# Attention values in three column blocks, ones on a sum of two key tiles, moves by DMA

## The chip, the cores and the metric

The kernel runs on one core of a Trainium2 chip. Its engines are TensorE (PE), VectorE (DVE), ScalarE (ACT), GpSimd (POOL) and SyncE (SP, which here only issues DMAs); each has its own queue and they meet by semaphores. The metric is the device time of one launch in microseconds, the median of several runs.

## The reference

A block of adaptive layer norm, causal attention and a mixture of experts on x of 4 x 2048 x 512, in fp32. Cut to what the change touches:

```python
h = _layernorm(x) * (1 + ca) + sa
qkv = h @ Wqkv.T + bqkv; q, k, v = split(qkv)      # 16 heads of 32 channels
q, k = _rope(q), _rope(k)
att = einsum('bhqd,bhkd->bhqk', q, k) / sqrt(32)
att = softmax(where(causal, att, -inf), axis=-1)
y = einsum('bhqk,bhkd->bhqd', att, v)
x = x + ga * (y @ Wo.T + bo)
h = _layernorm(x) * (1 + cb) + sb
x = x + gb * moe(h)                                # 48 of 128 experts kept, top 8
```

## The kernel before

A batch of 2048 tokens is worked through in three stages, and a loop runs over the 4 batches. **The front**: norm, projections of q, k and v with weights split in two fp32r parts (`W`), rotation; q and k go to DRAM (`qkd`), v to DRAM (`vd`) and for the first group of four heads to SBUF (`V`). **The stream**: attention of 16 heads, one after another. **Routing**: output projection (L1209), second norm, gates. At the end of the stream all five engines meet (`meet`, L568 by the helper), and again at the end of routing. After the last batch come the 48 experts.

In the stream the scores are computed transposed: 128 keys on the partitions, a chunk `j` of 512 queries in the columns. A head has four chunks; chunk j has 4(j+1) key tiles, so a head has 40 tiles, taken in 20 units of two. Each tile is one product into PSUM (L1160, with a mask product at the diagonal, L1163), one exponential on ACT into a ring `Pt` (L999), and one product with the values (L1181). Four heads share a group `g`: their results lie in four blocks of 32 partitions of `ot`. The denominators of the softmax come from ones that stand beside the values in `V`: `values_and_ones` gives 64 columns, 32 of values and 32 of ones. The first tile of a unit writes PSUM partitions 0 to 63, the second 64 to 127 (L1181).

At the end of a chunk ACT copies four blocks of 32x512: values and denominators of the first tiles straight to `ot` and `den`, those of the second tiles to `od` (L984 to L988); POOL adds `od` to them (L876, L877). At the end of a group DVE inverts `den` (L1442), POOL multiplies (L885) and SP stores `ot` to DRAM (`otd`). Beside this the maxima of the next head are found: a product per tile (L1136), a reduction on DVE (L1417, L1421), a transpose (L1141), and two rows of maxima that SP copies into the q operand (L661). They are needed by the scores of chunks 0 and 2. The last head of a batch has no next one, and so no maxima beside it.

The order is written out by hand in `stream()`: in step n every engine takes the score of unit n, the value of unit n-2, what is in `beside[n]` (maxima) and in `closing[n]` (copies, additions, inverses, scaling, `fold` and `widen`). `fold` multiplies the output weights by the gate (L858), `widen` adds the bias to two chunks of tokens `xc` (L866). SP has an order of its own, a loop over heads (L626 onwards): wait for the scores of the last head, 12 loads of the next (`stack`), row of maxima, stores, row of maxima, and after the last head the loads of attention and tokens for two output chunks (`load_attention`, L724, and `load_tokens`, L728).

Of the kernel before, what the change touches and what calls it, by code (L numbers as in the profile page):

```python
# [7 lines left out]
F32 = mybir.dt.float32  # L8
F32R = mybir.dt.float32r
BF16 = mybir.dt.bfloat16  # L10
# [5 lines left out]
P = 128  # L16
# [78 lines left out]
NPT = 8  # L95
# [4 lines left out]
def extent(j, k):  # L100

    r = max(k - TPC * j, 0)
    first = 0 if (j, k) == (0, 1) else r * P
    return first, (r + 1) * P - first if k >= TPC * j else 0

# [36 lines left out]
def stream():  # L142
# [27 lines left out]
    for n in range(NU * H):  # L170
        out.append(("score", *divmod(n, NU)))
        if n >= 2:
            out.append(("value", *divmod(n - 2, NU)))
        out += beside[n] + closing[n]
    for n in range(NU * H, NU * H + 16):
        if n < NU * H + 2:
            out.append(("value", *divmod(n - 2, NU)))
        out += closing[n]
# [3 lines left out]
NV, NPT_B = NU * H, 2 * NU * H  # L182
# [65 lines left out]
def adaln_block(nc, x, wqkv, bqk, bv, wo, bo, cT, wmod, gwT, o2n_col, o2n_row, wgu, wdn, cos, sin, kst, out):  # L248
    with ExitStack() as ctx:
# [13 lines left out]
        qkd = dram("qkd", [NB, NG, P, 4, T])  # L263
        vd = dram("vd", [NB, P, NT, NG * P])
# [19 lines left out]
        idbf = place("idbf", [P, P], BF16)  # L284
        mtbf = place("mtbf", [P, 2 * P], BF16)
# [11 lines left out]
        V_AT = at[0]  # L297
        V = place("V", [P, 2, NT, 6, HD], F32)
# [4 lines left out]
        PT_AT = at[0]  # L303
        Pt = place("Pt", [P, NPT, CH], F32)
        OD_AT = at[0]
        od = place("od", [P, 2, 2, CH], F32)
        den = place("den", [P, T], F32)
        ot = place("ot", [P, T], F32)
# [16 lines left out]
        rsA = place("rsA", [P, TPC], F32)  # L325


        at[0] = X_AT = PT_AT + 2 * NPT * CH
        xin = [place("xin0", [P, TPC, C], F32), xin1]
        assert at[0] <= OD_AT  # L330
# [6 lines left out]
        vst = [vst0, place("vst1", [P, TPC, NG * P], F32)]  # L337
# [8 lines left out]
        at[0] = V_END - 4 * NT * 6 * HD  # L346
# [39 lines left out]
        B1 = place("B1", [P, TPC, 6, P], BF16)  # L386
# [3 lines left out]
        assert at[0] <= X_AT  # L390


        at[0] = OD_AT
# [8 lines left out]
        posi = place("posi", [P, TPC, NEW], I32)  # L402
        hi = place("hi", [P, TPC, NEW], I32)
        lo = place("lo", [P, TPC, NEW], I32)
        assert at[0] <= FRONT_AT - 4 * T
# [51 lines left out]
        w_lower = sem("w_lower")  # L457
        cs_in = [sem("cs_in0"), sem("cs_in1")]
# [27 lines left out]
        o_norm = sem("o_norm")  # L486
        den_inv = sem("den_inv")
        ot_ready = sem("ot_ready")
# [82 lines left out]
        def o_part(h, j, odd, what):  # L571

            at = 2 * odd + (what + h) % 2
            return O[j % 2][at * HD:(at + 1) * HD, :]

        def values_and_ones(g, k, h):

            at = h // 2 * 3 + h % 2
            return V[:, g % 2, k, at:at + 2, :].rearrange("p a d -> p (a d)")

# [4 lines left out]
        def _(sp):  # L585
# [17 lines left out]
            wait_apart(sp, mod_out, 80)  # L603

            with sp.Fori(0, NB) as b:
# [30 lines left out]
                def slots_of(g, tiles, heads):  # L636

                    return ((V[:, g % 2, tiles, 0, :], heads[:, :, 0:HD]),
                            (V[:, g % 2, tiles, 2:4, :].rearrange("p t a d -> p t (a d)"), heads[:, :, HD:3 * HD]),
                            (V[:, g % 2, tiles, 5, :], heads[:, :, 3 * HD:P]))  # L640

                def store_values(j):

                    wait_apart(sp, s1_dve, N_DVE * b + EMPTIED["vproj", j, TPC - 1])
                    sp.dma_start(vd[b, :, TPC * j:TPC * (j + 1), :], vst[j % 2][:, :, :]).then_inc(v_out[j % 2], 16)
                    if j == 0:
                        wait_apart(sp, ones_set, 5 * b + 3)
# [1014 lines left out]
```

## Time and profile before

| | us |
|---|---|
| median of 3 runs | 4691.33 |
| lowest, highest | 4687.53, 4701.44 |
| the profiled execution | 4692.54 |
| its span, first to last instruction | 4690.7 |
| mean granted TensorE clock | 0.941 of 2.4 GHz |

The profile is one execution of the program. The span is shared by the engines; busy time of PE covers matmuls whose ends are modelled, and weight loads (PEld) overlap them. The chain of waits is followed back from the last instruction: at each step to what released it. Idle time of an engine outside that chain costs nothing. The names of DMAs and instructions are output<-input.

### The profile page before, as it was taken

The page shows a single profiled execution, that of the slowest core. Times are in us where ns is not written, and L with a number is a line of the kernel's source. Part 1 is how long each engine was busy: PE and PEld are TensorE (multiplying, and loading weights), DVE is VectorE, ACT ScalarE, POOL GpSimd, SP SyncE. Part 2 cuts the span into 40 slices and gives each one's busy share as a digit, 9 for nine tenths or more (in the row PEclk, how much of TensorE's full clock was granted, in tenths as well). Part 3 has the DMA queues.
Part 4 walks back from the last instruction along what each step waited for, and adds up shares of the span by engine and source line. Part 5 has one row for each costly group of instructions (what it writes and reads, how often), then busy time and mean ns, then how long its engine had stood idle before and what let it go on. Part 6 is the DMA issues. An engine that isn't in the chain of part 4 may idle for free.

```text
span 4690.7 us, 75544 instructions
## 1 busy us (share of the span) xinstructions
PE 4213.7 (90%) x18784; PEld 2336.3 (50%) x18784; DVE 2924.8 (62%) x5831; ACT 2293.1 (49%) x4294; POOL 1584.6 (34%) x1059
## 2 busy tenths in 40 slices
PE   4899999886899999886899999867899999859998
PEld 2744444345744444355644444346644444337776
DVE  3766666565756667475657766475666666465655
ACT  1347767622356677532267677422377676321111
POOL 3632223313622223314522223305522223304544
PEclk8989999997989999987899999988899999979999
DMA  4431222122432122123412222123422221229997
GB/s 138 147 112 57 57 66 71 52 88 89 161 86 64 46 58 70 58 97 113 157 49 66 62 69 57 64 96 115 147 52 66 66 65 42 93 75 248 259 253 196
DMA packets 325089, 460.75 MB, mean 98 GB/s; under 512 B 143540, under 2 KB 150836, under 8 KB 321972
## 3 DMA queue, kind: packets, MB, share of 16 engines
q1 hardware_dynamic: 303160, 397.48, 27.9%
q0 software_dynamic: 21504, 58.40, 5.3%
q8 instruction: 168, 2.75, 0.2%
q14 instruction: 257, 2.11, 0.1%
HBM read 292.99 MB, written 168.56 MB: 98 GB/s over the span
## 4 chain that ended last, share of the span: by engine, by line
PE 64%; issue 16%; POOL 6%; DMA 5%; DVE 4%; ACT 3%; SPq 1%; POOLq 1%; ACTq 0%; DVEq 0%
PE PS L1181 23%; PE PS L1136 14%; PE PS L1160 11%; PE PS L1283 3%; PE PS L1209 3%; DMA out<-z,it 2%; POOL qs L850 2%; PE PS L1294 2%; POOL t L847 2%; PE PS L1163 1%; ACT Pt L999 1%; POOL hTl L823 1%; PE PS L1222 1%; PE PS L1254 1%; PE PS L1120 1%
## 5 line engine op out<-in xcount | busy, mean ns | idle before, releaser
L999 ACT ACTIVATE Pt<-PS 128x512 f32<-128x512 f32 (+3 forms) x2560 | 1230.9, 533 | 778.6 <-PE PS L1163 401.0
L1421 DVE TENSOR_REDUCE part<-PS 128x1 f32<-128x512 f32 x1536 | 1019.3, 686 | 715.9 <-PE PS L1136 715.3
L1181 PE MATMUL PS<-Pt,V 128*64 128x512 f32 (+3 forms) x5120 | 1276.0, 560 | 0.0
L1136 PE MATMUL PS<-QK 96*128 96x512 f32 (+3 forms) x2560 | 865.1, 420 | 68.2 <-DVE part L1421 34.1
L876 POOL TENSOR_TENSOR ot<-ot,od 32x512 f32<-32x512 f32 x256 | 326.1, 1274 | 1726.1 <-ACT od L985 1726.1
L1160 PE MATMUL PS<-QK 97*128 97x512 f32 (+3 forms) x2560 | 828.0, 391 | 24.1 <-ACT Pt L999 9.4
L1136 PEld LDWEIGHTS PS<-QK 96*128 96x128 f32 x2560 | 396.2, 192 | 892.3 <-DVE part L1417 416.4
L1417 DVE CUSTOM_DVE_ANT_0 PS<-PS,consts 128x128 f32<-128x128 f32 (+3 forms) x1024 | 500.9, 495 | 145.8 <-PE PS L1136 142.8
L1160 PEld LDWEIGHTS PS<-QK 97*128 97x128 f32 x2560 | 481.2, 193 | 162.7 <-ACT Pt L999 56.4
L1181 PEld LDWEIGHTS PS<-Pt,V 128*64 128x64 f32 x5120 | 255.9, 135 | 311.9 <-issue 240.3
L1120 PE MATMUL PS<-hTu,W 128*128 128x512 f32 x1024 | 349.8, 425 | 18.3 <-POOL hTl L823 18.3
L877 POOL TENSOR_TENSOR den<-den,od 32x512 f32<-32x512 f32 x256 | 324.0, 1266 | 0.0
L1442 DVE RECIPROCAL den<-den 128x128 f32<-128x128 f32 x256 | 235.6, 936 | 101.8 <-POOL den L877 101.8
L956 ACT ACTIVATE qraw<-PS,bqg 128x512 f32<-128x512 f32 x128 | 87.2, 688 | 380.8 <-PE PS L1120 237.1
L1283 PEld LDWEIGHTS PS<-XT,Wg 128*96 128x96 f32 x1536 | 250.6, 164 | 26.6 <-issue 25.4
L1283 PE MATMUL PS<-XT,Wg 128*96 128x192 f32 x1536 | 259.1, 327 | 1.3 <-ACT XT L1045 1.3
L1209 PE MATMUL PS<-wot,otc 128*128 128x512 f32 x384 | 193.1, 643 | 64.9 <-POOLq L568 64.9
L1120 PEld LDWEIGHTS PS<-hTu,W 128*128 128x128 f32 x1024 | 209.6, 208 | 66.1 <-issue 19.6
L1163 PE MATMUL PS<-mtbf,idbf 128*128 128x128 bf16 (+1 forms) x1024 | 234.6, 237 | 0.0
L850 POOL TENSOR_TENSOR qs<-qs,cs 128x1024 f32<-128x1024 f32 x64 | 211.2, 3301 | 30.5 <-DVE qs L1397 30.5
L847 POOL TENSOR_TENSOR t<-qraw,cs 128x1024 f32<-128x1024 f32 x64 | 155.5, 2430 | 179.5 <-ACT qraw L956 179.5
L1120 PE MATMUL PS<-hTl,W 128*128 128x512 f32 x512 | 215.0, 420 | 0.0
(161 smaller groups left out, 4743.4 us busy)
## 6 DMA issues: line engine op xcount, KB each, us to landing
QK<-qkd SPq DMA_DIRECT2D x720, 128.0 KB, 3.0
qkd<-st SPq DMA_DIRECT2D x64, 1024.0 KB, 4.4
Wg<-wgu SPq DMA_DIRECT2D x48, 768.0 KB
Wd<-wdn SPq DMA_DIRECT2D x48, 384.0 KB
xin<-x SPq DMA_DIRECT2D x16, 1024.0 KB, 5.4
vd<-vst SPq DMA_DIRECT2D x16, 1024.0 KB, 6.0
table<-modd SPq DMA_DIRECT2D x64, 256.0 KB, 4.0
xc<-x SPq DMA_DIRECT2D x16, 1024.0 KB, 7.6
```

The source lines that it names most:

```text
L850: nc.gpsimd.tensor_tensor(qs[:, :, :], qs[:, :, :], table_of, ALU.mult).then_inc(rope_mul, 1)
L876: nc.gpsimd.tensor_tensor(ot[own, cols], ot[own, cols], od[own, nn % 2, 0], ALU.add)
L877: nc.gpsimd.tensor_tensor(den[own, cols], den[own, cols], od[own, nn % 2, 1], ALU.add).then_inc(o_norm, 1)
L999: nc.scalar.activation(Pt[:, t % NPT, first:CH], S2[t % NS2][:, first:CH], ACT.Exp, scale=SCALE).then_inc(exp_done, 1)
L1120: last = mm(bank, W[:, w, k, i, g * P:(g + 1) * P], (hTu, hTl)[h][:, j % 2, k], start=(k, w, h) == (0, *TERMS[0]), stop=(k, w, h) == (KT - ...
L1136: mm(s1[:, 0:w], QK[0:3 * HD, hh % 2, 0, qb * P:(qb + 1) * P], QK[0:3 * HD, hh % 2, 1, c * CH:c * CH + w], start=True, stop=True).then_inc ...
L1160: last = mm(S2[t % NS2][:, first:CH], QK[0:3 * HD + 1, hh % 2, 1, k * P:(k + 1) * P], QK[0:3 * HD + 1, hh % 2, 0, j * CH + first:(j + 1) * ...
L1181: last = mm(O[j % 2][2 * i * HD:2 * (i + 1) * HD, first:CH], values_and_ones(g, kb + i, hh % GH), Pt[:, (2 * n + i) % NPT, first:CH], star ...
L1209: last = mm(PS[:, t % 2], rows_of, wot[:, k, :], start=k == 0, stop=k == KT - 1)
L1283: last = mm(banks[i][:, q, :], Wg[:, u % HELD, k, o:o + HALF], XT[:, u % 2, k // 2, k % 2, :], start=k == 0, stop=k == KT - 1)
L1417: v.tensor_tensor_reduce(out=s1[:, 0:w], in0=s1[:, 0:w], in1=K[:, K_NEG + CH - w:K_NEG + CH], scale=1.0, scalar=-3e38, op0=ALU.add, op1=AL ...
L1421: v.reduce_max(part[:, qb, cc:cc + 1], s1[:, 0:w], AX.X).then_inc(s1_dve, 1)
```

## The change

A unit becomes a round. Its two value products have 32 columns each and write partitions 0 to 31 and 32 to 63 of the bank. POOL adds the two probability tiles into `Sm` (step `plus`, new), and one product with a tile of ones `onesv` writes the denominators to partitions 96 to 127; at the diagonal the columns that only the first tile has get a ones product of their own. `V` has no more ones in it. The value of a round stands three units behind its score (LAG) instead of two, and `Pt` has 12 places instead of 8. At a chunk's end ACT copies the whole bank to `od` in one instruction, and SP moves three blocks of 32 partitions to their rows: to `ot`, to a new `o1` (the second tiles) and to `den`. Per group and chunk POOL adds `o1` to `ot` (step `join`).

`Pt`, `Sm` and `o1` lie where `W` was. So the split weights are stored to DRAM (`wd`) once, before the loop over batches, and loaded back in each routing stage.

```diff
+SHAPES = ((2,) * 2, (2,) * 4, (2,) * 6, (2,) * 8)
-NPT = 8
+NPT, NSM, LAG = 12, 3, 3
@@ stream()
-        closing[n + 2].append(("copy", hh, j, 0))
-        closing[n + 3] += [("copy", hh, j, 1), ("add", hh, j)]
+        closing[n + LAG].append(("copy", hh, j))
         if hh % GH == GH - 1:
+            closing[n + 7].append(("join", hh // GH, j))
             for i in range(TPC):
-                closing[n + 6 + i].append(("inverse", hh // GH, j, i))
-            closing[n + 6 + TPC].append(("scale", hh // GH, j))
+                closing[n + 7 + i].append(("inverse", hh // GH, j, i))
+            closing[n + 7 + TPC].append(("scale", hh // GH, j))
+            due[NU * hh + DUE[r]].append(("value", hh, r))
+            beside[min(NU * hh + DUE[r] - LAG, NU * H - 1)].append(("plus", hh, r))
@@ sync, before the loop over batches
             wait_apart(sp, mod_out, 80)
+            wait_apart(sp, w_lower, 1)
+            sp.dma_start(wd, W[:, :, :, :, :].bitcast(F32)).then_inc(w_out, 16)
+            wait_apart(sp, w_out, 16)
@@ sync, values of the first group
-                    for slot_of, heads in slots_of(0, slice(TPC * j, TPC * (j + 1)), vst[j % 2][:, :, 0:P]):
-                        sp.dma_start(slot_of, heads).then_inc(v_out[j % 2], 16)
+                    sp.dma_start(V[:, 0, own, :], vst[j % 2][:, :, 0:P]).then_inc(v_out[j % 2], 16)
+                def move(hh, j):
+                    nn = NCH * hh + j
+                    own, cols = slice(hh % GH * HD, (hh % GH + 1) * HD), slice(j * CH, (j + 1) * CH)
+                    wait_apart(sp, o_free, NCH * H * b + nn + 1)
+                    for slot_of, whole in ((0, ot), (1, o1), (3, den)):
+                        sp.dma_start(whole[own, cols], od[slot_of * HD:(slot_of + 1) * HD, nn % 2]).then_inc(o_moved[nn % 2], 16)
@@ sync, loop over heads: after the 12 loads of the next head
+                    if hh >= 2:
+                        move(hh - 2, NCH - 1)
                     max_row(hh - 1, 1)
+                    move(hh - 1, 0)
...
+                    move(hh - 1, 1)
                     if hh < H:
                         max_row(hh, 0)
...
+                    move(hh - 1, 2)
...
+                move(H - 1, NCH - 1)
@@ sync, routing
+                sp.dma_start(W[:, :, :, :, :].bitcast(F32), wd).then_inc(w_in, 16)
@@ gpsimd
+                    elif kind == "plus":
+                        pool.wait_ge(exp_done, ...)
+                        if at >= NSM:
+                            pool.wait_ge(pv_done, ONE + NV * b + at - NSM + 1)
+                            nc.gpsimd.tensor_tensor(total, of[0][:, first:CH] if i == 1 else total, of[i][:, first:CH], ALU.add).then_inc(sum_done, 1)
+                    elif kind == "join":
+                        pool.wait_ge(o_moved[nn % 2], ...)
+                        nc.gpsimd.tensor_tensor(ot[:, cols], ot[:, cols], o1[:, cols], ALU.add).then_inc(joined, 1)
@@ scalar
-                            nc.scalar.activation(od[own, nn % 2, 0], o_part(hh % GH, j, 1, 0), ACT.Copy)
-                            nc.scalar.activation(od[own, nn % 2, 1], o_part(hh % GH, j, 1, 1), ACT.Copy).then_inc(o_free, 1)
-                            nc.scalar.activation(ot[own, cols], o_part(hh % GH, j, 0, 0), ACT.Copy)
-                            nc.scalar.activation(den[own, cols], o_part(hh % GH, j, 0, 1), ACT.Copy)
+                        nc.scalar.activation(od[:, nn % 2], O[j % 2], ACT.Copy).then_inc(o_free, 1)
@@ tensor
-                        for i in range(2):
-                            last = mm(O[j % 2][2 * i * HD:2 * (i + 1) * HD, first:CH], values_and_ones(g, kb + i, hh % GH),
-                                      Pt[:, (2 * n + i) % NPT, first:CH], start=kb == 0, stop=kb == TPC * j + 2)
+                        for i, k in enumerate(ks):
+                            mm(O[j % 2][i * HD:(i + 1) * HD, firsts[i]:CH], V[:, g % 2, k, h * HD:(h + 1) * HD], of[i][:, firsts[i]:CH],
+                               start=begins, stop=r == LAST_USE[j, i])
+                        if firsts[1] > firsts[0]:
+                            mm(O[j % 2][3 * HD:P, firsts[0]:firsts[1]], onesv[:, :], of[0][:, firsts[0]:firsts[1]], start=begins, stop=False)
+                        mm(O[j % 2][3 * HD:P, firsts[1]:CH], onesv[:, :], Sm[:, at % NSM, firsts[1]:CH], start=begins, stop=r == LAST_ROUND[j]).then_inc(pv_done, 1)
```

How instructions stand now, at three places. First PE's queue in a steady head, around a value step at the diagonal. Before (L1136 maxima, L1160 scores, L1181 values):

```order
L1136 MATMUL PS<-QK 128x512 [waits s1_dve]
L1159 REGISTER_ALU
L1160 MATMUL PS<-QK 128x512 [waits exp_done]
L1159 REGISTER_ALU
L1160 MATMUL PS<-QK 128x512 [waits exp_done]
L1181 MATMUL PS<-Pt,V 64x256 [waits exp_done]
L1181 MATMUL PS<-Pt,V 64x128
```

After (L1166 maxima, L1190 scores, L1214 values, L1217 and L1218 ones):

```order
L1166 MATMUL PS<-QK 128x512 [waits s1_dve]
L1189 REGISTER_ALU
L1190 MATMUL PS<-QK 128x512 [waits exp_done]
L1189 REGISTER_ALU
L1190 MATMUL PS<-QK 128x512 [waits exp_done]
L1199 REGISTER_ALU
L1214 MATMUL PS<-Pt,V 32x256 [waits sum_done]
L1214 MATMUL PS<-Pt,V 32x128
L1217 MATMUL PS<-Pt,onesv 32x128
L1218 MATMUL PS<-Sm,onesv 32x128
```

Two products of 64 columns gave way to four of 32 here (off the diagonal to three), and the step waits for POOL's sum, where it waited for the exponential.

Second SP's queue at the end of a batch, from its last wait for a head's scores. Before:

```order
L562 REGISTER_ALU [waits s2_ready]
L661 DMA QK<-mT 1x8x128 [waits mt_ready]
L710 ISA
L710 DMA table<-modd 128x512
L562 ISA
L724 DMA otc<-otd 128x512 [waits ot_out0]
L724 DMA otc<-otd 128x512 x2
L728 DMA xc<-x 128x4x512
L724 DMA otc<-otd 128x512 [waits ot_out1]
L724 DMA otc<-otd 128x512 x2
L728 DMA xc<-x 128x4x512
```

After, from the moves of the last head's last chunk:

```order
L595 REGISTER_ALU
L684 DMA ot<-od 32x512 [waits o_free]
L684 DMA o_87<-od 32x512
L684 DMA den<-od 32x512
L595 ISA
L760 DMA otc<-otd 128x512 [waits ot_out0]
L760 DMA otc<-otd 128x512 x2
L764 DMA xc<-x 128x4x512
L760 DMA otc<-otd 128x512 [waits ot_out1]
L760 DMA otc<-otd 128x512 x2
L764 DMA xc<-x 128x4x512
```

The loads of attention (`otc`) and tokens (`xc`) stood right behind the last row of maxima; now they stand behind the last move, which waits for the last head's copy.

Third POOL's queue at the same place. Before, from the additions of the last chunk (L876, L877), and after, from the last sum (L911); L866 and L896 widen the tokens, L885 and L925 scale:

```order
L876 TENSOR_TENSOR ot<-ot,od 32x512 [waits o_free]
L877 TENSOR_TENSOR den<-den,od 32x512
L864 REGISTER_ALU [waits o_norm]
L865 ISA [waits gabo]
L866 TENSOR_TENSOR xc<-xc,rows 128x2048 [waits c_in0]
L866 TENSOR_TENSOR xc<-xc,rows 128x2048 [waits c_in1,gabo,o_norm]
L884 ISA [waits o_norm]
L885 TENSOR_TENSOR ot<-ot,den 128x512 [waits den_inv]
```

```order
L911 TENSOR_TENSOR Sm<-Pt 128x128 [waits pv_done]
L924 ISA [waits joined]
L925 TENSOR_TENSOR ot<-ot,den 128x512 [waits den_inv]
L894 REGISTER_ALU
L895 ISA [waits gabo]
L896 TENSOR_TENSOR xc<-xc,rows 128x2048 [waits c_in0]
L918 TENSOR_TENSOR ot<-ot,o_87 128x512 [waits o_moved1]
L896 TENSOR_TENSOR xc<-xc,rows 128x2048 [waits c_in1,gabo]
L924 ISA [waits joined]
L925 TENSOR_TENSOR ot<-ot,den 128x512 [waits den_inv]
```

The additions are gone; the widening of the second chunk now stands behind the joining of the last one (L918), and the joining behind the widening of the first.

## Rows read from the trace of the kernel before

**Rows 1.** Page: busy time by engine, and the chain that ended last, by engine.
```profile
PE 4213.7 (90%) x18784; PEld 2336.3 (50%) x18784; DVE 2924.8 (62%) x5831; ACT 2293.1 (49%) x4294; POOL 1584.6 (34%) x1059
...
PE 64%; issue 16%; POOL 6%; DMA 5%; DVE 4%; ACT 3%; SPq 1%; POOLq 1%; ACTq 0%; DVEq 0%
```

**Rows 2.** Windows: us; busy PE, PEld, DVE, ACT, POOL (count); clock; DMA share; GB/s.
```profile
496.00:536.40 40.40, 40.35 (x178) 17.97 (x178) 24.31 (x60) 28.57 (x57) 10.03 (x8) 1.00 0.17 46
...
890.60:925.40 34.80, 32.80 (x135) 11.90 (x133) 13.92 (x22) 27.68 (x54) 12.64 (x11) 1.00 0.34 114
```

**Rows 3.** Chain of waits, 570 to 580 us: start, us, engine and line.
```profile
570.04 1.01 PE PS L1181 x4
...
571.94 0.58 PE PS L1181 x3
```

**Rows 4.** Timeline of PE from 945 us: start us, us, engine, line, op.
```profile
949.03 1.02 PE L1209 MATMUL PS<-wot,ot 128*128 128x512 f32 x2
...
952.47 1.02 PE L1209 MATMUL PS<-wot,ot 128*128 128x512 f32 x2
```

**Rows 5.** Groups by line and form: two weight loads of PE.
```profile
L1181 PEld LDWEIGHTS PS<-Pt,V 128*64 128x64 f32 x5120 | 255.9, 135 | 311.9 <-issue 240.3 <-ACT Pt L999 33.9
...
L1141 PEld LDWEIGHTS PS<-consts,mx 128*8 128x8 f32 x128 | 10.6, 83 | 88.4 <-issue 77.6 <-DVE mx L1427 10.8
```

**Rows 6.** Timeline of POOL, the folding of the output weights.
```profile
803.56 4.97 POOL L858 TENSOR_TENSOR wot<-wot,rows 128x512 f32<-128x512 f32 x4
```

**Rows 7.** Groups by line and form: one of four copies on ACT.
```profile
L985 ACT ACTIVATE od<-PS 32x512 f32<-32x512 f32 x256 | 150.9, 589 | 3.0
```

**Rows 8.** Timeline of PE in a batch's last head.
```profile
919.90 0.50 PE L1160 MATMUL PS<-QK 97*128 97x512 f32 x1 [0.38 <-ACT Pt L999]
```

**Rows 9.** Timeline of SP's queue in a steady head.
```profile
564.15 7.03 SPq L626 DMA_DIRECT2D QK<-qkd  x12
...
574.74 0.72 SPq L661 DMA_DIRECT2D QK<-mT  x1
```

**Rows 10.** Chain of waits at the program's start.
```profile
66.65 3.92 DMA out<-zrow
...
70.89 0.44 SPq L608
```

**Rows 11.** DMA issues: count, size, median us to landing.
```profile
wm<-wmod SPq DMA_DIRECT2D x1, 6144.0 KB, 17.7
...
qkd<-st SPq DMA_DIRECT2D x64, 1024.0 KB, 4.4
```

**Rows 12.** Chain of waits at the hand-over into the stream.
```profile
271.98 4.32 DMA V<-vst
```

**Rows 13.** Timeline of PE at the same place.
```profile
281.10 0.77 PE L1136 MATMUL PS<-QK 96*128 96x128 f32 x2 [4.21 <-DMA QK<-qkd]
```

**Rows 14.** Timeline of all engines at a batch's end.
```profile
925.40 2.36 PE L1181 MATMUL PS<-Pt,V 128*64 128x512 f32 x12
...
930.36 1.26 POOL L876 TENSOR_TENSOR ot<-ot,od 32x512 f32<-32x512 f32 x1 [3.77 <-ACT od L985]
...
933.08 8.95 POOL L866 TENSOR_TENSOR xc<-xc,rows 128x2048 f32<-128x2048 f32 x2 [0.24 <-POOL den L877]
...
941.98 1.26 POOL L885 TENSOR_TENSOR ot<-ot,den 128x512 f32<-128x512 f32 x1
```

**Rows 15.** Timeline of SP's queue, loads for the output stage.
```profile
899.23 1.31 SPq L724 DMA_DIRECT2D otc<-otd  x3
...
900.63 0.39 SPq L728 DMA_DIRECT2D xc<-x  x1
...
903.10 0.62 SPq L728 DMA_DIRECT2D xc<-x  x1
```

**Rows 16.** Line L728 (token loads) from 890 to 915 us.
```profile
DMA to landing us min/median/max: 7.6/8.7/9.8
```

**Rows 17.** Waits: PE for the row of maxima.
```profile
PE PS L1160 <- DMA QK<-mT: 0.6, 1, 0.6
```

More of the change, by code:

```diff
@@ L94 @@
 ENDS = [max(u for u in range(NU) if UNITS[u][0] == j) for j in range(NCH)]
-NPT = 8
+SHAPES = ((2,) * 2, (2,) * 4, (2,) * 6, (2,) * 8)
+ROUNDS = [(j, tuple(range(sum(shape[:r]), sum(shape[:r + 1])))) for j, shape in enumerate(SHAPES) for r in range(len(shape))]
+NR = len(ROUNDS)
+NPT, NSM, LAG = 12, 3, 3
 NS1 = NS2 = 3
@@ L104, in extent, with tile_at @@
     return first, (r + 1) * P - first if k >= TPC * j else 0
+def tile_at(j, k):
+    return 2 * j * (j + 1) + k
+FIRST_ROUND = [min(r for r in range(NR) if ROUNDS[r][0] == j) for j in range(NCH)]
+LAST_ROUND = [max(r for r in range(NR) if ROUNDS[r][0] == j) for j in range(NCH)]
+DUE = [tile_at(j, ks[-1]) // 2 + LAG for j, ks in ROUNDS]
+LAST_USE = {(j, i): r for r, (j, ks) in enumerate(ROUNDS) for i in range(len(ks))}
+N_SUM = sum(len(ks) - 1 for _, ks in ROUNDS)
+SUMS = [sum(len(ks) - 1 for _, ks in ROUNDS[:r + 1]) for r in range(NR)]
+ROUND_OF = {tile_at(j, k): r for r, (j, ks) in enumerate(ROUNDS) for k in ks}
 def front():
@@ L169, in stream, with moved @@
     out = []
[L170 to L177, printed above, removed]
+    for n in range(NU * H + 16):
+        if n < NU * H:
+            out.append(("score", *divmod(n, NU)))
+        out += due[n]
+        if n < NU * H:
+            out += beside[n]
         out += closing[n]
     return out
-NV, NPT_B = NU * H, 2 * NU * H
+NV, NPT_B = NR * H, 2 * NU * H
+def moved(nn):
+    return 16 * sum(3 for m in range(nn % 2, nn + 1, 2))
 STEPS = front() + stream()
@@ L284, in adaln_block @@
         idbf = place("idbf", [P, P], BF16)
+        onesv = place("onesv", [P, HD], F32)
         mtbf = place("mtbf", [P, 2 * P], BF16)
@@ L389, in adaln_block @@
         pos = place("pos", [P, TPC, NEW], F32)
-        assert at[0] <= X_AT
-        at[0] = OD_AT
+        posi = place("posi", [P, TPC, NEW], I32)
+        assert at[0] <= OT_AT
+        at[0] = SPARE_AT
+        B1 = place("B1", [P, TPC, 6, P], BF16)
         B2 = place("B2", [P, TPC, 6, 2, P], BF16)
@@ L485, in adaln_block @@
         o_free = sem("o_free")
-        o_norm = sem("o_norm")
+        sum_done = sem("sum_done")
+        joined = sem("joined")
+        o_moved = [sem("o_moved0"), sem("o_moved1")]
         den_inv = sem("den_inv")
-        ot_ready = sem("ot_ready")
+        ot_ready = [sem("ot_ready%d" % j) for j in range(NCH)]
         ot_out = [sem("ot_out%d" % j) for j in range(NCH)]
@@ L1176, in _ @@
-                        if kb == 0 and nn >= 2:
-                            pe.wait_ge(o_free, ONE + NCH * H * b + nn - 1)
-                        for i in range(2):
-                            first, _ = extent(j, kb + i)
-                            last = mm(O[j % 2][2 * i * HD:2 * (i + 1) * HD, first:CH], values_and_ones(g, kb + i, hh % GH),
-                                      Pt[:, (2 * n + i) % NPT, first:CH], start=kb == 0, stop=kb == TPC * j + 2)
-                        last.then_inc(pv_done, 1)
+                        _, hh, r = step
```

156 lines of the change are left out of this document (74 added, 82 removed).

## The prediction

> **What bounds the kernel now.** I read the page first: TensorE (PE) is busy for 90% of a span of 4690.7 us and the chain of waits lies on it for 64% [rows 1]. That is a mean over stages, so the windows come next. In a steady head of the attention stream (one head is 20 units of two key tiles and takes 40.4 us; there are 16 heads and 4 batches) PE is busy for 40.35 of 40.40 us at full clock (2.4 GHz), while ScalarE (ACT) works 28.57 and GpSimd (POOL) 10.03 [rows 2]. Only the last head of a batch, which has no maxima to find beside it, leaves PE idle: 32.80 of 34.80 us [rows 2]. So in 15 of 16 heads a change pays only if it takes columns, loads or array changes from PE. The chain inside one head shows what a unit costs: a value group with 512 columns holds the chain for 1.01 us, one with 256 and 128 columns for 0.58 [rows 3]. Around the stream other things set the end: the start of the program, the hand-over into the stream, and the end of each batch, where all engines meet.
>
> **The value products.** Before, the two tiles of a unit go to two blocks of 64 columns side by side (values and ones in one product). After, they go to two blocks of 32, and a third block of 32 takes ones times the sum of the two probability tiles. Does that cut streaming? An fp32 product of 512 columns is two instructions; four such products with the whole array take 3.43 us from the start of one row to the next but one, 0.86 each [rows 4]. A unit's two products take 1.01 together, so the two blocks already run side by side and only 0.15 us is load and change of shape. A third block beside them saves no column. What gets shorter is the first weight load: 8 columns take 83 ns and 64 take 135 [rows 5], 0.93 ns per column, so 32 fewer save 30 ns. Against that stand the start of a third block (two more instructions and two more loads) and, in 7 of 20 units, a split of the ones product at the diagonal. No row shows a third block. From below: nothing added, -30 ns a unit. From above: the second block, the load and the change of shape cost 0.15 together, so +0.07 if a further block takes half of that. I take +16, since a unit of 1.01 leaves little that a second block can have cost, so -14 ns net. Times 20 x 64 = 1280 units: **-18 us** (-38 to +90).
>
> The Trainium skill weighs here ("TensorE: Matmul & The Clock Gate", "Measured speedup vs the span model"): further blocks add about 4 ns each, but the same table gives three column blocks 2.38 times the speed of one, not 3. No row has three blocks; two agree with the first figure. By the first, the estimate for this term would be -33 us; by the second a unit would take 3/2.38 of 0.86, which is 1.08, and the term would be +90 us (estimate).
>
> **The sums.** 20 additions per head on POOL, of 128x512 where the unit is off the diagonal. Four POOL products of that shape take 4.97 us [rows 6], 1.24 each, so at most 25 us a head beside PE's 40.4; the 8 additions of 32 rows that go took 10. The product of unit n now stands three units later instead of two, so a sum has nearly two units (4 us) for its 1.24: hidden. The reductions on DVE read PSUM. Once a batch the folding of the output weights occupies POOL for 4.97 + 1.24 us [rows 6], three units; the sums behind it come about half a microsecond late: **+2 us** over four batches (0 to 6).
>
> **The copies.** Per chunk four ACT copies of 32x512 at 589 ns [rows 7] become one of 128x512, which takes as long: 7 us of ACT less per head. In a steady head PE idles 0.05 us, so nothing comes of it. In the last head PE waits for the exponentials behind these copies, seven times, 0.2 to 0.4 us; one of them is [rows 8]. All 2.0 us of idle time [rows 2] may go: **-8 us** for four batches (0 to -12).
>
> **The moves.** 12 more DMAs per head on SP's queue. The 12 loads of the next head take SP 7.03 us from 564.15 [rows 9], 0.59 each, so it is past them at 571.2. The value group at 570.04 [rows 3] will be the one that closes the previous head; its copy, behind two exponentials, is done near 572. Three moves at 0.59 last until 573.8, and the row of maxima for which SP waits next is issued at 574.74 [rows 9]. They fit with 0.9 us to spare: 0.
>
> **Start of the program.** The split weights are now written to DRAM once (6144 KB), after zeroing is done, and SP waits for that before it loads any input. The chain runs through SP at just this place: it waits 3.92 us for the DMA on `out`, and at 70.89 issues the first input [rows 10]. Nothing hides it. The load of the same size took 17.7 us; a write of 1024 KB takes 4.4 [rows 11], which six times over is 26, and 15 if 2 us of each are fixed. **+18 us**, once. Reading it back comes after the meeting, where its space is free and the next use is a whole routing stage away: 0.
>
> **Hand-over into the stream.** SP stores the last values with four DMAs, waits for all, and only then loads head 1. The last of the three DMAs with small elements ends that chain, 4.32 us to land [rows 12], and PE idles 4.21 us [rows 13]. Now it is one DMA with 512 byte pieces. I take 1.5 us each time: **-6 us** (0 to -12).
>
> **End of each batch.** This is the largest term. Before, from the last value product (ends at 925.40 + 2.36 = 927.76): copies, two additions, then POOL adds the bias to two token chunks (8.95 us), scales the last chunk and all engines meet; 941.98 + 1.26 is 15.5 us after the product [rows 14]. The tokens had been loaded 30 us earlier, issued at 900.63 and 903.10 [rows 15]. After, SP must issue the moves of the last head first; the attention and token loads stand behind the very last move (SP's order shows it). Counted from the last product: copy 0.7, SP and three moves 1.7 to 1.9, so the first attention load is issued at 2.4. From there the first tokens land 1.40 + 7.6 = 9.0 later [rows 15, 16]: 11.4. Widening one chunk, 4.47 [rows 14]: 15.9. Joining, 1.24: 17.1. Second widening (its tokens land at 2.4 + 3.87 + 9.8 = 16.1): 21.6. Scaling, 1.26: 22.9. Against 15.5 that is +7.4, four times: **+30 us** (20 to 40). What had been covered by POOL's own work, the tokens' landing, becomes the wait that ends last.
>
> **Sum.** -18 + 2 - 8 + 18 - 6 + 30 = +18. Own time of the profiled execution 4692.5 (1.8 outside the span); it lies 1.2 above the median of 4691.33. Forecast 4710.5, so **4710 us**, 0.4% slower. About 0.3% (14 us) is what a measurement can tell from no change: 4677 to 4705 counts as the same.
>
> **Rivals.**
> *The third block does not run fully beside the others.* The array takes the third block's columns in turns: three blocks take 1.5 times two. Place: every value group. 16 units of 512 columns at +0.43 us and 4 of 256 at +0.21 give 7.7 us a head, 493 in all: 5200 us. A milder form (+0.07 a unit, the upper bound above) gives 4710 + 108 = 4818. (The page's 2.38 would be this form.) For it: no row has three blocks. Against: two run together at no visible price. Chance 0.08 and 0.06.
> *Faster: the change of shape gets cheaper too.* The 0.15 us of a unit is load and drain. If both shrink with the columns of a block, half of it, 75 ns a unit, goes: -96 instead of -18, so 4632. Place: again the value groups. It decides from 28 ns a unit (36 us of other terms over 1280). For it: only the 0.15 that the rows leave unexplained. Against: the load of 64 columns is 60 ns of it at 0.93 each [rows 5], and a wait for the array to drain need not know columns. With a part of it, 4660 to 4690. Chance 0.15.
> *A new wait in the stream.* The row of maxima that SP sends at 574.74 is needed by the first score of the third chunk, four units after the score that precedes the group at 570.04 [rows 3], so near 577.5; it held PE once already, for 0.6 us [rows 17]. If the moves take longer to issue than the loads, or their packets delay its landing, PE waits 0.5 to 1 us in 60 heads: +30 to +60, so 4740 to 4770. Chance 0.16.
> *Forecast as written:* 0.55, with 4692 to 4730 as its own range.
>
> **Numbers.** Below 4677: most of the second rival, 0.11. From 4677 to 4705: its rest and a quarter of the forecast's case, in which the two large losses are nearer their lower bounds, 0.27. Above: 0.62. The range leaves out the first rival in both forms and the far end of the second: 4678 to 4790.
>
> **What would show it.** Value groups of 512 columns near 1.00 us in the chain (rival one: 1.08 to 1.43). PE in a steady head still above 99% busy, period 40 us. In the last head no wait of PE for ACT. First input DMA issued near 89 us instead of 71. From the last value product to the last scaling 23 us instead of 15, with POOL's wait before the first widening put down to the DMA of the tokens. A wait of PE for the row of maxima would show the third rival. I am wrong if the value groups shrink by more than 28 ns or grow.

## The result, and the profile after

The changed kernel takes **4715.71 us** (median of 11 runs, 4704.89 to 4726.96); the kernel before, on the same chip, 4694.53 (11 runs, 4687.53 to 4703.12). The ratio is 1.0049 [1.0037, 1.006], so it is slower, by about half a per cent. The profiled spans are 4710.5 and 4690.7: 19.8 us to account for; the medians are 21.2 apart. The page after, answering [rows 1], busy time and the chain:

```profile
PE 4168.9 (89%) x22240; PEld 2362.4 (50%) x22240; DVE 2910.1 (62%) x5832; ACT 1818.7 (39%) x3526; POOL 2378.9 (51%) x1883
...
PE 67%; issue 15%; POOL 8%; DVE 4%; DMA 3%; ACT 1%; SPq 1%; POOLq 1%; DVEq 0%; ACTq 0%
```

ACT lost 474 us of work, POOL took 794, and PE, which counts, lost 45. The windows answer [rows 2]: a steady head, then the last head of the first batch.

```profile
496.00:536.40 40.40, 40.16 (x238) 18.51 (x232) 24.48 (x62) 21.42 (x46) 21.46 (x20) 1.00 0.27 70
901.80:934.00 32.20, 31.51 (x190) 12.24 (x188) 14.04 (x22) 20.31 (x42) 23.46 (x22) 1.00 0.14 34
```

Read the second number against the first: PE still fills a steady head to 99.4%, and in the last head it now idles 0.7 us where it idled 2.0.

To place the 19.8 us, take three kinds of instants from PE's timeline in each batch: the first transposes, the last score and the first output product. The first column below is when the program's first transposes start; the next two are means of the four batches, from a batch's first score to its last (the stream), and from there to the first output product (the end of the batch). "Routing" is all that follows the first output product, summed over batches, the experts at the program's end included. Each kernel is told of below. The four stage columns come from one profiled execution of each kernel, which lies up to 15 us from its median; each ratio is to the kernel before on the same chip.

| kernel | start | stream | end of batch | routing, sum | median us | ratio to before |
|---|---|---|---|---|---|---|
| before | 82.5 | 662.8 | 18.9 | 1162 | 4694.5 | |
| after | 99.0 | 655.5 | 28.5 | 1157 | 4715.7 | 1.0049 [1.0037, 1.006] |
| e1, loads before the moves | 99.2 | 666.0 | 16.3 | 1161 | 4704.5 | 1.0026 [1.0016, 1.0036] |
| e2, start without the wait | 83.7 | 655.5 | 28.0 | 1172 | 4709.4 | 1.0033 [1.0021, 1.0046] |
| e3, four blocks | 98.8 | 657.8 | 28.1 | 1153 | 4722.5 | 1.0075 [1.0061, 1.0089] |
| e4, ones once a chunk | 98.7 | 653.1 | 27.8 | 1166 | 4708.4 | 1.0036 [1.0022, 1.005] |
| e5, loads between the moves | 99.2 | 655.7 | 18.0 | 1163 | 4680.8 | 0.9973 [0.9963, 0.9984] |
| e6, two tiles, repaired | 83.4 | 656.0 | 14.3 | 1163 | 4650.3 | 0.9908 [0.9893, 0.9924] |
| e7, three tiles | 99.4 | 631.3 | 32.9 | 1147 | 4625.4 | 0.9859 [0.9843, 0.9876] |
| e8, three tiles, repaired | 83.2 | 629.9 | 17.4 | 1163 | 4568.2 | 0.9734 [0.9721, 0.9747] |
| e9, joins on DVE | 83.1 | 653.3 | 19.5 | 1161 | 4669.6 | 0.996 [0.9945, 0.9975] |
| e10, joins later | 83.6 | 631.2 | 17.9 | 1172 | 4570.5 | 0.9754 [0.9737, 0.9772] |

After against before: start +16.5, four streams -29.1, four ends +38.4, routing -5.5, the stages before the streams -0.5; sum +19.8. The change works where it was aimed and pays for it at the edges.

**Start.** The chain there, answering [rows 10]:

```profile
66.66 3.89 DMA out<-zrow
70.70 15.93 DMA wd<-W
```

**Value groups.** The chain of waits in a steady head, start and duration; one group, first the first of the two instructions of each product, then the second:

```profile
511.61 0.55 PE PS L1214 x2
512.16 0.01 PE PS L1218
512.17 0.42 PE PS L1214 x2
512.59 0.01 PE PS L1218
```

The four pieces make 0.99 us against the 1.01 of [rows 3]. The blocks of 32 (L1214 values, L1218 ones) lie over each other, and no column is paid for twice. The first load, answering [rows 5], takes 27 ns less:

```profile
L1214 PEld LDWEIGHTS PS<-Pt,V 128*32 128x32 f32 x5120 | 184.8, 108 | 333.5 <-issue 204.8 <-POOL Sm L911 48.3 <-ACT od L1017 43.6
```

Counted from one group's first weight load to the next instruction's, in twelve steady heads of each batch, the median group of 512 columns went from 1009 to 989 ns, one split at the diagonal from 1009 to 994, the narrow one from 576 to 568. One narrow group in each head takes 0.88 us after the change, because the product behind it waits 0.3 us for DVE; the scores near it take 0.3 us less than before. The steady heads as wholes went from 40.49 to 40.16 us (medians), which agrees with the medians of the groups.

**End of a batch.** The timeline answers [rows 14, 15]. Follow it down: last sum, last value product, copy, three moves, and only then the loads.

```profile
936.21 1.28 POOL L918 TENSOR_TENSOR ot<-ot,o 128x512 f32<-128x512 f32 x1
937.44 0.47 POOL L911 TENSOR_TENSOR Sm<-Pt 128x128 f32<-128x128 f32 x1
937.96 0.40 PE L1214 MATMUL PS<-Pt,V 128*32 128x256 f32 x2 [0.57 <-POOL Sm L911]
938.66 0.60 ACT L1017 ACTIVATE od<-PS 128x512 f32<-128x512 f32 x1 [3.90 <-PE PS L1218]
940.53 0.59 SPq L684 DMA_DIRECT2D den<-od  x1
942.82 0.39 SPq L764 DMA_DIRECT2D xc<-x  x1
949.81 4.49 POOL L896 TENSOR_TENSOR xc<-xc,rows 128x2048 f32<-128x2048 f32 x1 [10.68 <-DMA xc<-x]
954.26 1.26 POOL L918 TENSOR_TENSOR ot<-ot,o 128x512 f32<-128x512 f32 x1
955.47 4.49 POOL L896 TENSOR_TENSOR xc<-xc,rows 128x2048 f32<-128x2048 f32 x1
959.92 1.26 POOL L925 TENSOR_TENSOR ot<-ot,den 128x512 f32<-128x512 f32 x1
961.90 2.90 PE L1244 MATMUL PS<-wot,otc 128*128 128x512 f32 x3 [23.30 <-POOLq L601]
```

From the last value product's end (938.6) to the last scaling's end (961.2) is 22.6 us, forecast at 22.9. What I had not counted is at the top: the join of chunk 2 (936.21) stands in POOL's queue ahead of the last sum, so the last value product itself comes late (it waits 0.57 us, and its weight load 1.26). From the last score to its end, 2.7 us became 4.7.

### The profile page after: what moved, and what is told of

Read it like the earlier page. It is cut to its first block, busy times and chain, and to the rows that moved or that the text cites. A ratio compares the mean times of both kernels' runs of the same rounds, so it can differ in the third digit from the quotient of the medians.

```text
span 4710.5 us, 86803 instructions
## 1 busy us (share of the span) xinstructions
PE 4168.9 (89%) x22240; PEld 2362.4 (50%) x22240; DVE 2910.1 (62%) x5832; ACT 1818.7 (39%) x3526; POOL 2378.9 (51%) x1883
## 3 DMA queue, kind: packets, MB, share of 16 engines
q14 instruction: 282, 2.31, 0.2%
## 4 chain that ended last, share of the span: by engine, by line
PE 67%; issue 15%; POOL 8%; DVE 4%; DMA 3%; ACT 1%; SPq 1%; POOLq 1%; DVEq 0%; ACTq 0%
PE PS L1214 21%; PE PS L1166 15%; PE PS L1190 11%; PE PS L1318 5%; PE PS L1329 3%; PE PS L1244 3%; POOL qs L884 3%; PE PS L1218 2%; POOL t L881 2%; PE PS L1193 1%; POOL hTl L859 1%; PE PS L1257 1%; PE PS L1289 1%; PE PS L1304 1%; DMA xc<-x 1%
## 5 line engine op out<-in xcount | busy, mean ns | idle before, releaser
L911 POOL TENSOR_TENSOR Sm<-Pt 128x512 f32<-128x512 f32 (+2 forms) x1280 | 1370.6, 1074 | 1054.8 <-PE PS L1218 833.4
L1214 PE MATMUL PS<-Pt,V 128*32 128x512 f32 (+3 forms) x5120 | 1242.5, 547 | 7.4 <-POOL Sm L911 7.0
L1218 PE MATMUL PS<-Sm,onesv 128*32 128x512 f32 (+2 forms) x2560 | 1130.6, 524 | 0.0
L1166 PE MATMUL PS<-QK 96*128 96x512 f32 (+3 forms) x2560 | 866.6, 420 | 88.3 <-DVE part L1457 33.9
L1190 PE MATMUL PS<-QK 97*128 97x512 f32 (+3 forms) x2560 | 808.2, 388 | 13.7 <-DVE vst L1426 8.7
L1166 PEld LDWEIGHTS PS<-QK 96*128 96x128 f32 x2560 | 398.0, 192 | 839.4 <-DVE part L1453 351.4
L1190 PEld LDWEIGHTS PS<-QK 97*128 97x128 f32 x2560 | 478.4, 194 | 121.7 <-ACT Pt L1028 38.4
L1150 PE MATMUL PS<-hTu,W 128*128 128x512 f32 x1024 | 349.2, 424 | 17.9 <-POOL hTl L859 17.9
L1214 PEld LDWEIGHTS PS<-Pt,V 128*32 128x32 f32 x5120 | 184.8, 108 | 333.5 <-issue 204.8
L951 POOL DMA_INDIRECT out<-z,it x96 | 139.3, 1451 | 213.2 <-issue 128.8
```

What stands on the lines that cost most here:

```text
L911: nc.gpsimd.tensor_tensor(total, of[0][:, first:CH] if i == 1 else total, of[i][:, first:CH], ALU.add).then_inc(sum_done, 1)
L1150: last = mm(bank, W[:, w, k, i, g * P:(g + 1) * P], (hTu, hTl)[h][:, j % 2, k], start=(k, w, h) == (0, *TERMS[0]), stop=(k, w, h) == (KT - ...
L1166: mm(s1[:, 0:w], QK[0:3 * HD, hh % 2, 0, qb * P:(qb + 1) * P], QK[0:3 * HD, hh % 2, 1, c * CH:c * CH + w], start=True, stop=True).then_inc ...
L1190: last = mm(S2[t % NS2][:, first:CH], QK[0:3 * HD + 1, hh % 2, 1, k * P:(k + 1) * P], QK[0:3 * HD + 1, hh % 2, 0, j * CH + first:(j + 1) * ...
L1214: mm(O[j % 2][i * HD:(i + 1) * HD, firsts[i]:CH], V[:, g % 2, k, h * HD:(h + 1) * HD], of[i][:, firsts[i]:CH], start=begins, stop=r == LAS ...
L1218: mm(O[j % 2][3 * HD:P, firsts[1]:CH], onesv[:, :], Sm[:, at % NSM, firsts[1]:CH], start=begins, stop=r == LAST_ROUND[j]).then_inc(pv_done, 1)
```

## The experiments

### e1: the loads before the last head's moves

```diff
                     max_row(hh - 1, 1)
+                    if hh == H:
+                        for j in range(2):
+                            load_attention(j)
+                            load_tokens(j)
                     move(hh - 1, 0)
...
                 move(H - 1, NCH - 1)
...
-                for j in range(2):
-                    load_attention(j)
-                    load_tokens(j)
```

> SP issues the attention and token loads of the first two chunks in the last head ahead of that head's first moves, not behind its very last one; nothing else changes. Theory (the end of a batch grew by 28.5 - 18.9 = 9.6 us because the tokens land late): the first widening no longer waits for them. From the last score: last value product 4.7, then copy and moves to 9.3 (2.4 us and 2.0 to land), join 1.3, scaling 1.3, but POOL's two widenings of 4.5 each stand in front of them as in the kernel before, so about 19 to 20 us to the first output product, 8.5 less per batch, 34 in all: 4680 us. Rival (the three moves with their own 2 us landing, and the joins, are what ends last, not the tokens): 2 to 3 us per batch at most, 4705 to 4710.

Measured: 4704.5. The end of a batch fell by 12.2 us, below that of before. But the last head grew from 32.1 us (first to last score) to 40.1 to 45.1. The line of the moves from 905 to 945 us (who waited for it, and its time to landing), then a row of PE's waits there:

```profile
its engine sat idle before it (us, times) until:
who waited for it (us, times):
  DVE den L1480: 25.6, 2
  POOL ot L919: 9.0, 1
...
DMA to landing us min/median/max: 1.9/4.6/10.3
```
```profile
PE PS L1215 <- POOL Sm L912: 7.7, 1, 7.7
```

The moves of 64 KB landed in up to 10.3 us instead of 2.0: they stood behind 3.5 MB of loads (two chunks of 1024 KB of tokens and 768 KB of attention; the expectation of e5 miscounts them as 2.8). POOL's join waited 9.0 for them, the sums stood behind the join, and PE waited 7.7. The clock then cost more. Windows of 10 us around and behind that wait (the second number is PE's busy time, the third from the end the granted clock):

```profile
925.00:935.00 10.00, 2.31 (x8) 0.32 (x8) 4.33 (x6) 1.09 (x2) 3.85 (x4) 0.66 0.44 133
935.00:945.00 10.00, 10.00 (x36) 3.51 (x36) 2.93 (x4) 4.65 (x9) 7.50 (x6) 0.50 0.08 20
```

PE was busy for 2.31 of 10 us, and all of the next 10 us ran at 1.2 GHz (0.50). So a wait of 7.7 us goes with a head that is 13 us longer. The median of 4704.5 lies at the rival's edge, but not by the rival's mechanism: the end of a batch fell by 12.2, not by 2 to 3. That the tokens' landing is what ends last is the theory's; e5 shows it without the longer head. Why the place was wrong, neither had.

### e5: the loads between the moves

The same four lines, behind `move(hh - 1, 1)`.

> The loads of attention and tokens for the first two chunks stand behind the last head's moves of its second chunk (in the queue of SP), so that the moves of the first two chunks land ahead of them. Theory (what ends last at the end of a batch is the landing of the tokens, and e1 lost 8 to 15 us in the last head only because three moves stood behind 2.8 MB in the same DMA queue): stream 655.5 us as in the changed kernel, last score to first output product 16 to 17 us instead of 28.5; 12 us x 4 = 48, 4668 us. Rival (any 2.8 MB in the last head holds the moves up and with them POOL's joins and sums): the stream grows by 8 us or more again, 4700 us or above.

Measured: 4680.8, faster than before. The stream is 655.7, as in the changed kernel, and the end of a batch 18.0, 10.5 less (12 forecast). This one edit of order turns the change from a loss of 0.5% to a gain of 0.3%, which is small but clear of its interval. The rival's first half does show: the moves still behind the loads landed in up to 6.4 us. No join and no sum of POOL waited for them, though, so the rival is out.

### e2: the start without the wait

```diff
-            sp.dma_start(wd, W[:, :, :, :, :].bitcast(F32)).then_inc(w_out, 16)
-            wait_apart(sp, w_out, 16)
...
                 sp.dma_start(bvg[:, :], bv.rearrange("g p -> (g p)").partition_broadcast(P)).then_inc(bv_in, 16)
+                sp.dma_start(wd, W[:, :, :, :, :].bitcast(F32)).then_inc(w_out, 16)
...
+                wait_apart(sp, w_out, 16 * (b + 1))
                 sp.dma_start(W[:, :, :, :, :].bitcast(F32), wd).then_inc(w_in, 16)
...
+                            if t == 0:
+                                act.wait_ge(w_out, ONE + 16 * (b + 1))
```

> The 6144 KB write of the split weights is issued behind the first input loads of a batch, in every batch, and ScalarE waits for it before the first exponential instead of SP at the program's start. Theory: the start gets its 16 us back (first transposes at 83 instead of 99 us), nothing else moves: 4700 us. Rival (the transfers share bandwidth, the write delays the second input or the stores of the first parts in each of four batches): part of the 16 is given back, up to 10 us per batch, and it comes out between 4700 and 4740.

Measured: 4709.4. The first transposes start at 83.7, 15.3 us earlier, and streams and ends are as they were; the stages before the streams too (718.9 against 718.5 us, summed over batches), so the rival's delay isn't there. Of the forecast 16 us, 6 came in the medians and 1.2 in the profiled executions. What is missing there lies in the routing stage, where this edit adds one wait of SP for a write that had long landed: 1172 against 1157 us. The windows of that stage in the first batch, of after and of e2:

```profile
961.90:1133.20 171.30, 123.20 (x617) 80.22 (x617) 110.27 (x222) 39.15 (x60) 16.07 (x9) 0.83 0.37 131
```
```profile
947.90:1121.90 174.00, 125.17 (x617) 80.82 (x617) 114.42 (x222) 39.29 (x60) 16.06 (x9) 0.81 0.38 133
```

The same 617 instructions run at a mean granted clock of 0.83 and 0.81. Over the twelve kernels the routing sum lies between 1147 and 1172 us, so much of this is scatter that comes with the clock. It isn't shown that the edit has no part in it: the five kernels that carry it (e2, e6, e8, e9, e10) have sums of 1161 to 1172, the seven others 1147 to 1166. That stays open.

### e3 and e4: a block more, a block less

```diff
+                        for slot_at in (2, 3):        # e3: both get ones times the sum
...
+                        if begins:                    # e4: ones in a chunk's first group alone
```

> Each value group gets a fourth block: ones times the sum once more, into the 32 partitions that nobody reads. Theory (a block beside others costs only its start and its load, 16 us ns-scale as in the prediction, +16 ns a unit): group of 512 columns 989 to about 1005 ns, 16 x 1280 ns = +20 us, 4736 us. Rival of turns (blocks share the array's input): +0.43 us a group of 512, +493 us, above 5200; its mild form +0.07 us a unit, 4805. If the fourth block costs nothing at all, 4716.

> Leaves out the denominators: ones are multiplied in the first group of each chunk only (with constant data), so 16 of the 20 groups per head have two blocks of 32 columns and nothing else. Theory (load term -30, third block +16): these groups fall from 989 to about 973 to 979 ns, 10 to 16 ns x 1024 groups = 10 to 16 us less, 4700 to 4705. Rival A (the third block costs nothing, the gain is all load or something else): 989 stays, 4716. Rival B (the third block costs as much as a share of the columns): over 50 ns a group, under 4665.

Measured: 4722.5 and 4708.4 (4736 and 4700 to 4705 forecast); median group of 512 columns 996 ns with four blocks, 989 with three, 982 with two. The chain of e4 has the group in one piece, for the reader to compare with the pieces of after:

```profile
508.40 0.98 PE PS L1214 x4
```

(The 16 in the expectation of e3 are ns.) The medians are counted from weight load to weight load, as above. e4 leaves out most of the denominators. Streams grew by 2.3 us with the fourth block and fell by 3.0 to 4.2 in three batches of e4; its second batch was 0.8 longer, with three heads 0.3 to 1.6 us above those of the others. So a block beside others costs **7 ns**, not 16. And two blocks of 32 take 27 ns less than before's two blocks of 64: exactly the difference of the two weight loads, 135 to 108. Nothing is left for a drain that would depend on the columns of a block. Both forms of turns (+0.43 and +0.07 us) are excluded, and so is the faster rival. The two figures of the Trainium skill ("TensorE: Matmul & The Clock Gate", "Measured speedup vs the span model") part here: its 4 ns for a further block is the nearer one, and low against the 7 measured, and its 2.38 times for three blocks doesn't show in this kernel, where the measured group of 989 decides against the 1080 that it would give.

### e6: both repairs, and the second widening behind the meeting

> The edit of e5, the edit of e2 (write of the split weights behind the first input loads, waited for by ScalarE), and the widening of the second token chunk moved behind the meeting of the engines. Theory: 48 from the tokens, 16 from the start, and 4.5 x 4 = 18 from the widening, which stands on POOL ahead of the last join and scaling: 4716 - 82 = 4634 us. Rival (the last moves, 2.4 us behind the last value product and 2.0 to land, set the end once the tokens are early, and the widening hides behind them): 4640 to 4652.

Measured: 4650.3. The last edit takes 3.7 us off each end of a batch (18.0 to 14.3; 4.5 forecast). Of the 82 us, 65 came; 9 are missing from the ends (57 instead of 66), 6 are in the routing stage, 2 lie in the streams. The total is in the rival's range, but its mechanism doesn't show in the first batch: POOL begins the last join as soon as it is done with the first widening, and doesn't wait for the moves. That first widening still stands ahead of the join.

### e7 and e8: three key tiles in a group

If a block costs 7 ns, the fourth quarter of the array stands empty for nothing. A third tile in a group saves whole groups.

```diff
-SHAPES = ((2,) * 2, (2,) * 4, (2,) * 6, (2,) * 8)
+SHAPES = ((2, 2), (3, 3, 2), (3, 3, 3, 3), (3, 3, 3, 3, 2, 2))
...
+        o2 = place("o2", [P, T], F32)
-                    for slot_of, whole in ((0, ot), (1, o1), (3, den)):
+                    for slot_of, whole in ((0, ot), (1, o1), *([(2, o2)] if j else []), (3, den)):
```

> Value groups of three key tiles where the chunk has enough of them: 15 groups per head instead of 20, with a fourth block (third tile) in 10 of them, one more sum per group on POOL (25 per head), one more move per chunk and one more addition at the end; the row of maxima is sent ahead of the previous head's last moves. Theory (a block beside others costs 7 ns, a group 0.98 us): per head 16 groups of 0.99 and 4 of 0.57 become 11 of 1.00, one of 0.79 and 3 of 0.57, 18.1 to 13.5, so 4.6 x 64 = 297 us less, 4419 us. Rival A (PE no longer bounds: POOL's 25 sums of 1.07 and ScalarE's 40 exponentials in 35.6 us make PE wait half a microsecond or more in every third group): 4480 to 4560. Rival B (the row of maxima comes too late for a head of 35.6 us): 1 to 2 us a head, 4480 to 4540.

> The groups of e7 with the three repairs of e6. Theory: the two gains add, 4419 - 82 = 4337 us. Rival (with the shorter last head the loads of the tokens collide with the moves, as in e1): up to 8 us per batch of it is lost, 4370 us.

Measured: 4625.4 and 4568.2; **e8 is 2.7% faster than the kernel before**. A clear gain, but e7 brought 90 us where 297 were forecast, less than either rival allowed; e8 brought 57 of its 82. The value groups did shrink as worked out: median 996 ns at 512 columns, 14.0 us of them per head against 18.4. Heads fell only from 40.2 to 37.1, and those in which a group of heads closes (numbers 3, 7 and 11, counted from 0) to between 39.9 and 42.5. Windows of e8, an ordinary head and the one from 403 us, in which a group closes:

```profile
497.00:534.10 37.10, 36.12 (x218) 17.34 (x210) 23.81 (x61) 20.86 (x44) 27.08 (x25) 1.00 0.31 78
403.00:440.00 37.00, 34.08 (x195) 15.98 (x194) 28.87 (x64) 19.08 (x39) 32.49 (x28) 0.95 0.24 63
```

In the first PE idles 1.0 us: groups are fewer, the scores and maxima between them as many, and PE waits for the banks that DVE empties and for the row of maxima. In the second POOL works 32.5 of 37.0 us, nearly without a gap from 411 to 439, with the sums of the group behind its joins and scalings. DVE is nearly as full in places. Two windows of 5 us of that head, and two of the last head of the same batch:

```profile
425.00:430.00 5.00, 3.05 (x17) 1.22 (x15) 4.79 (x10) 2.67 (x5) 4.92 (x4) 0.98 0.37 106
430.00:435.00 5.00, 5.00 (x20) 2.24 (x20) 2.09 (x4) 1.49 (x3) 4.84 (x5) 0.68 0.01 2
```
```profile
880.00:885.00 5.00, 1.23 (x8) 0.48 (x10) 0.00 (x0) 2.42 (x5) 4.84 (x5) 0.88 1.04 390
885.00:890.00 5.00, 5.00 (x19) 1.02 (x18) 1.59 (x2) 1.09 (x2) 4.84 (x5) 0.50 0.42 120
```

In the closing head PE waits 1.3 us for POOL's sum and 0.9 for DVE, and then runs in part at 1.2 GHz (mean clock 0.68). In the last head it waits 7.4 us for POOL's sums, in five waits, with POOL full, and then has half the clock. So the last head took 35.8 to 36.1 us at a mean clock of 0.89 to 0.91, where it took 32.1 at full clock in the changed kernel. My rivals named POOL for every head and the clock for none; POOL binds in the last head, and with DVE in the three closing ones. The end of a batch is longer too (32.9 against 28.5): the last value product ends 7.2 us behind the last score, not 4.7. e8 gives back 15.5 of each end and 16 at the start, but its routing stage was 16 longer than e7's. The collision that its rival names doesn't show: its last heads took as long as e7's.

### e9 and e10: POOL relieved in the closing heads

> e8 with the seven joining additions of each group's last head on VectorE (DVE) instead of POOL. e8's heads 3, 7 and 11 took 40.0 to 41.1 us where the others took 37.1, and POOL stood busy without a gap from 411 to 439 us. Theory (in those heads POOL is the bound: 25 sums, 7 joins and 4 scalings): 7 x 1.27 = 9 us leave POOL, those heads fall to 37.5 to 38.5 (10 us per batch less at most), and the last head and the tail lose 1 to 3 us per batch: 4568 - 35 = 4533 us, 4515 to 4550. Rival (DVE's joins wait for the moves in front of the maxima, whose banks PE then waits for): the heads stay at 40, 4560 to 4575.

> e8 with the joins, reciprocals and scalings of the first three groups two to three units later (chunks 1 to 3), still on POOL; the last group is left as it is. Theory (POOL is the bound for some 25 us of heads 3, 7 and 11, and its work can be carried into the next head, where it has half a microsecond to spare in each unit): half of the 3 us in each comes back, 4 us a batch, 4552 us. Rival (the sum of POOL's work over the stretch decides, not its place): no change, 4568.

Measured: e9 4669.6, a loss of 101 us against e8 (the kernel before differs by 1 us between their two chips) and far outside what either side expected. Windows of e9:

```profile
410.00:420.00 10.00, 9.29 (x61) 4.50 (x57) 8.06 (x18) 5.59 (x12) 7.72 (x6) 1.00 0.35 86
420.00:430.00 10.00, 7.82 (x43) 3.58 (x35) 9.94 (x17) 4.62 (x9) 8.01 (x8) 0.94 0.12 29
430.00:440.00 10.00, 9.72 (x44) 4.17 (x45) 7.42 (x15) 4.03 (x9) 7.78 (x8) 0.72 0.08 28
```

DVE is full (9.94 of 10 us): reciprocals of 0.94 each stand beside the maxima already, and the seven additions come on top. PE waits for its banks, 7.82 busy; in the window after, its granted clock is 0.72, a mixture of 2.4 and 1.2 GHz, and 44 matmuls fill 9.72 us. PE waited 2.2 us, and the lower clock took another 2.8 of 10 us of full speed (estimate, from the 0.72): the wait is paid twice. Heads 3, 7 and 11 and the ones behind them took 42.3 to 46.8 us. The last head, which has no maxima, did gain (36.0 to 33.0 in the mean). The additions themselves were dear:

```profile
L1477 DVE TENSOR_TENSOR ot<-ot,o x16: 681/1133/2516, 415.9 to 925.4; 128x512 f32<-128x512 f32 x16
```

The rival was right in kind. e10: 4570.5, no change, as its rival said. Heads 3 and 4 together fell by 1.3 us in each batch; heads 7 and 8 together rose by 1.6 to 7.1, where the one head of 45.9 us ran at a mean clock of 0.83. So moving POOL's work gave nothing in all; that its sum alone decides isn't shown, since the clock changed with it.

## Why the prediction was right

It was right in the total (4710 forecast, 4715.7 measured) and in the sign of the terms that matter; the sizes, by its own steps:

- **Value groups, -18 forecast.** Measured about -21: 13 groups of 512 columns a head at -20 ns, 3 split ones at -15, 4 narrow ones at -8, 0.34 us a head. The load was -27 (forecast -30), the block +7 (forecast +16; shown by e3 and e4), the split 5. The mechanism held; the block was mis-sized by half.
- **Sums, +2.** The head with the folding took 41.0 us, once 42.6, against 40.5 before: +3.6 in all, and about +5 beside the 0.34 us that its value groups save. PE waits there for POOL's sum 1.2 us, where the four folds (4.99) stand ahead of it.
- **Copies, -8.** The last head went from 35.2 to 32.1 us, first to last score; 0.3 of that is the value groups, so about -11. The waits for ACT are gone, [rows 8] among them, as forecast. But the idle time fell by only 1.3 us a head; the other 1.5 lie in time that counts as busy, which I hadn't seen could shrink. No run takes the copies out alone.
- **Moves, 0.** Landing 2.0 us and no wait of PE for them in a steady head. In the last head PE now waits 0.7 to 0.8 us for the row of maxima, which SP issues behind three moves, in each batch (it is counted in the -11 above), and once in another head, 1.0. Before, it waited once in the program, 0.6, and in no last head. That is the third rival, in small: 3.8 us. e1 shows that this holds only while nothing large is ahead of them.
- **Start, +18.** Measured +16.5. The write took 15.9 us to land, near the lower of my two bounds (15 and 26); six times 2.4 and the fixed 2 us once are 16.4.
- **Hand-over, -6.** About -1 (the first heads took 2.3 us less in all, 1.3 of it by their value groups). This step failed. I took the three small-element DMAs as the reason for 4.32 us [rows 12]. The one DMA now takes longer to land:

```profile
285.47 6.54 DMA V<-vst
```

In both kernels it stands behind the 1024 KB store of all values, issued 0.4 us ahead of the first of these DMAs, which lands in 5.9 us before and 6.1 after. From the issue of that store to the landing of the last values it is 7.3 us before and 7.0 after: so the store ahead, and not the size of the elements, looks like what sets this; no run takes the store away. PE idles 6.08 us before head 1's first maxima instead of 4.21 [rows 13], because it comes to that wait 2.6 us earlier, counted from the batch's first transposes.
- **End of a batch, +30.** Measured +38.4. Behind the last value product the working held within 0.4 us. The missing 2 us per batch lie ahead of it: my step on the sums asked whether one lies beside PE's work in a steady head, and not what stands in POOL's queue ahead of the last one.

The stages sum to +19.8 where I had +18; three errors of size (ends +8, hand-over +5, sums +3) were met by gains in groups, copies and the start, and by a routing stage 5.5 us shorter, within the 25 us by which that sum scatters. That the total came so near is in part luck. Of the rivals, turns and the cheaper change of shape are excluded by e3 and e4. The late row of maxima cost 3.8 us, not 30 to 60.

## What to carry to other kernels

When a change takes work off the bound engine, list what now stands in front of what in the in-order queues at each edge of the stage; here 29 us gained inside the stream were lost to 38 at its ends, and moving four load calls by a few lines turned the sign. A column block beside others is nearly free on this array, so the number of groups, not the number of blocks, is what to cut, until the engine that prepares their operands fills up: in e8 PE then waited, and ran at half clock behind the waits.

## What the runs showed of the hardware

- Narrow blocks of fp32 products run side by side up to four at once: 982, 989 and 996 ns for two, three and four blocks of 32 columns, 512 streamed.
- Small transfers behind large ones on SP's queue land late: 2.0 us became up to 10.3 behind 3.5 MB, and behind a store of 1024 KB the last of 256 KB of values landed 7.0 us after the store's issue as one DMA with 512 byte pieces, 7.3 as three with smaller ones.
- In e1 a wait of PE of 7.7 us was followed by 10 us at 1.2 GHz. In e9 a stretch of 10 us in which PE waited for 2.2 was followed by one with a mean granted clock of 0.72; in e8 PE was busy 3.05 of 5 us, its longest wait 1.3 us, and the next 5 us ran at 0.68. In the routing stage the same instructions took 166.6 to 174.0 us at mean clocks of 0.86 to 0.81.
- One form of addition on DVE (128x512, fp32, both operands in SBUF) took from 0.68 to 2.52 us, while POOL worked beside it. What makes the difference wasn't tested.
